# Attention and mixture of experts on one core: the causal mask moves into the row-maximum pass of the vector engine, the values' constant to the GpSimd engine

## The reference, cut to what matters

```
xa  = x @ (W_attn + lora)^T ; normalised over all tokens (batch norm), then split into q, k, v
att = softmax(causal(q k^T / sqrt(128)))
x   = LayerNorm(x + att v @ W_proj^T @ (W_proj + lora)^T)
gates = the two largest router probabilities of LayerNorm(x), made to sum to 1
x   = LayerNorm(x + sum over the two experts e of gate_e * (gelu(LN_e(x) W1_e + b1_e) W2_e + b2_e))
```

## Time and profile before

| what | value |
|---|---|
| median of 3 runs | 430.78 us (429.72 to 431.52) |
| profiled execution, its own time | 431.83 us |
| its span | 430.1 us |
| mean granted clock of PE | 0.985 |
| PE busy | 408.5 us (95%) |
| DVE busy | 282.9 us (66%) |
| ACT busy | 323.7 us (75%) |
| POOL busy | 321.0 us (75%) |

### The profile page before, as it was taken

The page is one execution under the profiler, slowest core; times in us unless marked ns, Lnnn a source line. Parts: engine busy times, 40 slices in busy tenths (PEclk is TensorE's granted clock), DMA queues, the critical chain, the costliest instruction groups (busy, mean ns, idle before and its releaser), DMA issues.

```text
span 430.1 us, 14555 instructions
## 1 busy us (share of the span) xinstructions
PE 408.5 (95%) x3490; PEld 390.8 (91%) x3490; DVE 282.9 (66%) x1612; ACT 323.7 (75%) x830; POOL 321.0 (75%) x606
## 2 busy tenths in 40 slices
PE   7998899999998999999999999999999999999980
PEld 7967787999887999999999999999999999999980
DVE  2446677899999677656555555446766666666663
ACT  1226788999988678877888888888888888888751
POOL 7000276888888888888887787748878888788885
PEclk9999999999999899999999999999999999999995
DMA  9999411111113532454543355542333333333211
GB/s 236 323 402 378 117 41 34 42 45 48 42 47 115 123 85 85 127 148 137 138 128 108 98 166 155 161 139 72 106 101 105 111 108 109 108 83 101 69 32 37
DMA packets 45490, 51.69 MB, mean 120 GB/s; under 512 B 6610, under 2 KB 37074, under 8 KB 45410
## 3 DMA queue, kind: packets, MB, share of 16 engines
q1 hardware_dynamic: 37312, 31.46, 27.0%
q0 software_dynamic: 7728, 18.51, 12.7%
q10 hardware_dynamic: 370, 0.80, 0.6%
HBM read 28.23 MB, written 21.72 MB: 116 GB/s over the span
## 4 chain that ended last, share of the span: by engine, by line
PE 65%; POOL 13%; issue 12%; DVE 5%; ACT 1%; DMA 1%; POOLq 0%; SPq 0%; DVEq 0%; ACTq 0%
PE bank L880 19%; PE bank L895 18%; POOL r_z L603 7%; POOL out L609 6%; PE bank L686 3%; PE bank L740 3%; PE bank L870 3%; PE bank L726 2%; PE bank L761 2%; PE bank L677 2%; PE bank L749 1%; PE bank L770 1%; PE bank L772 1%; PE bank L751 1%; PE bank L750 1%
## 5 line engine op out<-in xcount | busy, mean ns | idle before, releaser
L880 PE MATMUL bank<-xT 128*128 128x128 f32 x1136 | 152.1, 277 | 0.0
L895 PE MATMUL bank<-w2T,xT 128*128 x1136 | 150.2, 275 | 0.6 <-DVE yt L1476 0.6
L895 PEld LDWEIGHTS bank<-w2T,xT 128*128 128x128 f32 x1136 | 138.2, 192 | 0.8 <-issue 0.8
L880 PEld LDWEIGHTS bank<-xT 128*128 128x128 f32 x1136 | 138.7, 193 | 0.0
L932 ACT ACTIVATE xT<-w1T,zero_col 128x512 f32 x139 | 100.4, 722 | 41.2 <-issue 37.5
L1476 DVE TENSOR_TENSOR yt<-bank,b_bc 128x128 f32<-128x128 f32 x142 | 41.4, 291 | 92.7 <-PE bank L895 87.6
L609 POOL DMA_INDIRECT out<-xT,xg x71 | 75.9, 1069 | 17.1 <-issue 17.1
L596 POOL DMA_INDIRECT queue<-xT,xg x71 | 72.0, 1014 | 20.1 <-POOL idle L594 16.2
L1069 ACT ACTIVATE xT<-bank 128x512 f32<-128x512 f32 x142 | 82.0, 577 | 2.4 <-PE bank L880 2.4
L575 POOL DMA_INDIRECT queue<-x_all x64 | 62.2, 972 | 12.6 <-issue 7.9
L932 ACT ACTIVATE xT<-bank,one_col 128x128 f32<-128x128 f32 x142 | 52.1, 367 | 10.9 <-PE bank L870 4.8
(11 more groups left out here) (238 smaller groups left out, 740.1 us busy)
## 6 DMA issues: line engine op xcount, KB each, us to landing
xg<-queue SPq DMA_DIRECT2D x71, 129.5 KB, 2.2
xg<-queue SPq DMA_DIRECT2D x71, 67.5 KB, 2.0
x_all<-x SPq DMA_DIRECT2D x16, 256.0 KB, 6.1
xT<-x_t SPq DMA_DIRECT2D x8, 512.0 KB, 9.9
w1r<-w_t SPq DMA_DIRECT2D x8, 256.0 KB, 5.8
w2T<-w_t SPq DMA_DIRECT2D x8, 256.0 KB, 11.5
queue<-xT,xg POOLq DMA_INDIRECT x71
out<-xT,xg POOLq DMA_INDIRECT x71
```

Of the source, the lines that this page charges most:

```text
L880: last = mm(bank[2 + s][:, h * P:(h + 1) * P], w1c[:, (q - 1) % WR, h * P:(h + 1) * P], xgT[:, s, :], start=True, stop=True)
L895: last = mm(bank[4 + s][:, 0:P], hs[:, s, h, :], w2T[:, bass.ds(e, 1), h, :].rearrange("p a d -> p (a d)"), start=(h == 0), stop=(h == HC ...
```

## The change

Four things are changed.

1. **The mask.** PE's `start_scores` goes away. The three score products now start their own sums. `row_max` on DVE becomes two `tensor_tensor_reduce`: each adds a f32 mask tile to the scores, turns the sign, writes the result to the new SBUF tile `masked`, and takes its minimum, which is the negated row maximum. ACT's exponentials read `masked` with scale -1 and no longer PSUM. `scores(b)` waits for `row_max(b-2)`, no longer for the exponentials of b-2.
2. **The constant.** PE's `start_v` goes away. Of `cv` only the 8 router columns still go by PE: after each of the two value products a bf16 product of 8 columns with the matrix of ones. The 128 value columns are added by POOL to x's rows (`add_constant`, one `tensor_tensor` of 128 columns for each tile): for batches 0 to 17 in one go ahead of the first scatter, for batch b+18 in the scatter of batch b, one ahead of each of its two DMAs, where the memset is then 128 columns in place of 384 (batches 14 to 31 keep 384). DVE's residual waits for it (`s_xa`). The three splits of the constant are 8 columns wide and all stand ahead of `row_max(0)`.
3. **The router's logits.** Two `tensor_tensor` over both tiles become one `scalar_tensor_tensor` for each tile, both ahead of the statistics.
4. **The gate.** ACT's `gate` moves into `roots`, between the logarithms and the wait for them.

```diff
-            def start_v(b):
-                wait(pe, s_vs, b)
-                mm(bank[1][:, 0:TPB * (E + VW)], ones_b[:], cv3[:], start=True, stop=False)
-            def start_scores(b):
-                wait(pe, s_p, b - 1)
-                mm(bank[2 + b % 2][:, 0:2 * P], ident_b[:], mask_b[:], start=True, stop=False)
             def make_v(b):
+                wait(pe, s_vs, b)
                 for t in range(TPB):
-                    last = mm(bank[1][:, t * (E + VW):(t + 1) * (E + VW)], xT[:, b * T + t * P:b * T + (t + 1) * P],
-                              wvvT[:], start=False, stop=(t == TPB - 1))
+                    at = t * (E + VW)
+                    mm(bank[1][:, at:at + E + VW], xT[:, b * T + t * P:b * T + (t + 1) * P], wvvT[:], start=True,
+                       stop=False)
+                    last = mm(bank[1][:, at:at + E], ones_b[:], cv3[:], start=False, stop=True)
                 last.then_inc(s_v, 1)
             def scores(b, s):
                 pe.wait_ge(s_zs, b + 1)
+                wait(pe, s_mx, b - 1)
...
+            ADD_FIRST = 18
+            def add_constant(b, t):
+                row = x_all[:, b * TPB + t, DATA:DATA + P]
+                return pool.tensor_tensor(row, row, cv[:, E:VW], ALU.add)
...
-            def part_transfers():
+            def part_transfers(b, t):
                 pg.settle()
-                pg.did(pool.memset(idle[:, 0:3, :], 0.0))
+                later = b + ADD_FIRST
+                if later < NB:
+                    last = add_constant(later, t)
+                    if t == TPB - 1:
+                        last.then_inc(s_xa, 1)
+                    pg.did(pool.memset(idle[:, 0, :], 0.0))
+                else:
+                    pg.did(pool.memset(idle[:, 0:3, :], 0.0))
...
+            pool.wait_ge(s_cv, 1)
+            for b in range(ADD_FIRST):
+                add_to_batch(b)
...
-                v.tensor_reduce(nmax[:, s, 0:1], bank[2 + s][:, 0:P], AXX, ALU.max, negate=True)
-                v.tensor_reduce(nmax[:, s, 1:2], bank[2 + s][:, P:3 * P], AXX, ALU.max, negate=True).then_inc(s_mx, 1)
+                v.tensor_tensor_reduce(masked[:, s, 0:P], bank[2 + s][:, 0:P], mask[:, 0:P], -1.0, -MASKED, ALU.add,
+                                       ALU.min, nmax[:, s, 0:1])
+                v.tensor_tensor_reduce(masked[:, s, P:3 * P], bank[2 + s][:, P:3 * P], mask[:], -1.0, -MASKED, ALU.add,
+                                       ALU.min, nmax[:, s, 1:2]).then_inc(s_mx, 1)
...
+            def logits(b, t):
+                op(v.scalar_tensor_tensor(out=lg[:, t, :], in0=x_cols(b, t, 0, E), scalar=x_cols(b, t, ROOT, ROOT + 1),
+                                          in1=r_bias[:], op0=ALU.mult, op1=ALU.add))
```

More of the change, by code:

```diff
@@ L489, in _ @@
             pg.did(pool.memset(zero_col[:], 0.0))
-            pg.did(pool.memset(mask_b[:], 0.0))
+            pg.did(pool.memset(mask[:], 0.0))
             pg.did(pool.iota(iota_e[:], [[1, E]], base=0, channel_multiplier=0, allow_small_or_imprecise_dtypes=True))
@@ L824, in attend_step @@
                     rank(k - 4)
-                if has[-1]:
-                    start_v(ahead)
-                    start_scores(ahead)
                 if has[1]:
@@ L975, in roots @@
                                scale=1.0 + EPS_FFN).then_inc(s_ln, 1)
+                if gated is not None:
+                    gate(gated)
                 act.wait_ge(s_ln, b + 1)
@@ L1023, in attend_step @@
                 if has[2]:
-                    roots(k - 2)
-                if has[4]:
-                    gate(k - 4)
+                    roots(k - 2, k - 4 if has[4] else None)
             def gate(b):
@@ L1233, in residual @@
                 last.then_inc(s_mv6, 1)
+            def logits(b, t):
+                op(v.scalar_tensor_tensor(out=lg[:, t, :], in0=x_cols(b, t, 0, E), scalar=x_cols(b, t, ROOT, ROOT + 1),
+                                          in1=r_bias[:], op0=ALU.mult, op1=ALU.add))
             def route(b):
                 v.wait_ge(s_rr, b + 1)
-                op(v.tensor_tensor(lg[:], x_all[:, of_batch(b), 0:E],
-                                   x_all[:, of_batch(b), ROOT:ROOT + 1].to_broadcast([P, TPB, E]), ALU.mult))
-                pg.settle()
-                op(v.tensor_tensor(lg[:], lg[:], r_bias[:].unsqueeze(1).to_broadcast([P, TPB, E]), ALU.add))
+                for t in range(TPB):
+                    logits(b, t)
                 pg.settle()
@@ L1263, in first_steps @@
                 row_max(0)
-                for n in range(1, 3):
-                    split_constant(n)
-                v.sem_inc(s_cv, 1)
                 row_max(1)
@@ L1296, in attend_step @@
                     v.wait_ge(s_rr, b3 + 1)
-                    op(v.tensor_tensor(lg[:], x_all[:, of_batch(b3), 0:E],
-                                       x_all[:, of_batch(b3), ROOT:ROOT + 1].to_broadcast([P, TPB, E]), ALU.mult))
+                    for t in range(TPB):
+                        logits(b3, t)
                     made_lg = pg.n
@@ L1301, in attend_step @@
                     v.wait_ge(s_yr, b2 + 1)
-                    op(v.bn_stats(st6[:, 0, :], x_row(b2, 0)))
-                if has[3]:
-                    pg.settle(made_lg)
-                    op(v.tensor_tensor(lg[:], lg[:], r_bias[:].unsqueeze(1).to_broadcast([P, TPB, E]), ALU.add))
-                    made_lg = pg.n
-                if has[2]:
-                    op(v.bn_stats(st6[:, 1, :], x_row(b2, 1)))
+                    for t in range(TPB):
+                        op(v.bn_stats(st6[:, t, :], x_row(b2, t)))
                     made_st = pg.n
```

54 lines of the change are left out of this document (26 added, 28 removed).

## The result

The change makes the kernel slower: 439.53 us (438.65 to 440.83, 6 runs) against 431.05 (429.72 to 431.84, 6 runs), a ratio of 1.0215 [1.0197, 1.0234]. The profiled execution took 439.34 us, its span is 437.6 us, 7.5 more than before. The forecast was 431.6 with 427.5 to 434.5, so it was wrong in its size, in its sign and in its range.

A forecast was written before the change was run, and what follows sets the result against it. PE was taken to bound attention in steps 6 to 10 and 13 to 20, DVE in 21 to 27. Profiled: 431.83 + 0.9 - 0.2 + 0.15 = 432.7; median: 430.78 + 0.85 = 431.6 us, range 427.5 to 434.5.

The forecast's parts named there:

- PE's step: PE in attention: 0.23 us removed, 0.05 and 0.24 added, net +0.06 us a step, +0.9 us over about 16 steps.
- the transposes behind the ranks: PE, each step: their first weights become uncovered, priced at 0.08 us like the other two places, without a row.
- The rival of covered weights: PE pulls f32 weight loads ahead of the small products: step 2.75 us, kernel faster at 427.6 us; chance 0.24.
- DVE has 2.98 - 2.70 = 0.28 us a step to hide it: Attention steps that PE sets: DVE's added cost stays hidden behind PE, with 0.28 us a step of room.
- steps 6 to 10: Early attention steps with PE full at 4.06 us a step: counted among those PE lengthens by 0.06 us each.
- POOL's addition: One addition of 128 columns on POOL takes 0.45 us, between 0.35 and 0.63.
- DVE's own cost: DVE: fused row maximum and logits (taken as 0) net +0.02 us a step; +0.15 us over 7 DVE-set steps.
- the step that failed: POOL before the first scatter: 36 additions take 16 us (13 to 23) while it has no work; scatter late by nothing.
- The signs that I had named for being wrong: Attention trace after: PE not full in steps 13 to 20, or its step there below 2.85 us.
- Three narrow splits ahead of `row_max(0)`: Start of attention: they replace one wide split, beside PE's first scores; cost 0, between -0.3 and +0.3 us.
- The rival had the mechanism: POOL additions and DVE's two-SBUF-operand operations block each other: 434.5 us at 0.6 us a step, at most 437; chance 0.15.
- Lateness: POOL's scatters about 3 us late (at most 9), covered by 19 us: 0; rival of later experts, 5 us or more, 0.02.

The follow-up runs named there:

- tiny_last: The whole change with only 8 batches' additions first, begun behind the splits, and both 8-column products behind both value products; 443.73 us, ratio 1.003 on the second chip.
- gaps_tt: The whole change with a wait behind each of the 36 first additions and the two old logits operations; 434.15 us, ratio 1.0094 to the kernel before.
- no_first: The whole change without POOL's 36 first additions (constant left out of batches 0 to 17); 433.92 us, ratio 1.0085 to the kernel before.
- first8_tt: The whole change with old logits and only 8 batches' additions first, begun behind the splits, the others in 24 batches' scatters; 437.56 us, ratio 1.0195.
- full_again: The whole change, unaltered, run once more on the third chip; 439.75 us, ratio 1.0222 to the kernel before.
- tt_logits: The whole change with the two old tensor_tensor operations for the logits; 441.41 us, ratio 1.0266 to the kernel before.

## Why the prediction was wrong

**PE's step: the mechanism right, one term too high, and PE not alone.** Forecast 0.06 us a step more in steps 13 to 20 and a period of 2.98. Most periods there are 2.95 to 2.96 (2.92 to 2.93 before), so +0.03; three are longer (3.12, 3.01 and 3.02), and with them the piece z(14) to z(22) has grown by 0.53, 0.07 a step. That the total agrees with the forecast is in part luck. The starts in the timeline of after give the terms: the 8-column products take 0.03 each, as priced; the second value product and the first score product, each behind a small one, 0.08 more, as priced; but the transposes behind the ranks take 0.36 to the next start in place of 0.33, so 0.03 where I had put 0.08 without a row. The rival of covered weights (0.24) falls. That PE sets these steps is not shown any more: DVE has no idle time there either, and in tiny_last 0.08 a step less on PE gave 0.01. "DVE has 2.98 - 2.70 = 0.28 us a step to hide it" failed there. In steps 6 to 10 they gained 0.29 in place of losing 0.3: the fold of one expert's matrix, which nobody edited, takes 0.86 us from L697 to L698 where it took 0.94 (60.10 to 61.04, L677 to L678, before). Why is open; with the mask's part alone it is still 0.93.

**POOL's addition: right in itself.** Forecast 0.45 us (0.35 to 0.63). It is 437 ns in the mean, and in the string 0.39 (14.06 us for 36).

**DVE's own cost: the mask as forecast, the logits at the upper bound.** The fused operations cost 0.03 to 0.04 us a step (3.99 us in the seven steps of z(22) to z(29), 3.72 before) for a forecast of +0.02. The logits I took as 0 between -0.04 and +0.08. In after the pair takes 0.27 us from start to next start (115.83 to 116.10), where the two before took 0.18, 0.19 in the mean: 0.57 us in seven steps, the whole upper bound. The two make 0.8 us where the sum had 0.15. The rest of the 1.10 us by which z(22) to z(29) has grown is mostly where the cut falls: the list's long reduction, 1.12 us to the next start, lies wholly behind z(22) in after, and before only 0.67 us of it did.

```profile
102.69 1.20 DVE L1391 TENSOR_REDUCE n_h<-oh_all 128x16 f16<-128x576 f16 x1
```

```profile
110.78 1.21 DVE L1394 TENSOR_REDUCE n_h<-oh_all 128x16 f16<-128x576 f16 x1
```

The old logits, in gaps_tt, take 0.54 us less there than the new ones in after, but the piece is only 0.15 shorter: the list's casts and the statistics take more.

**The start: the step that failed.** "In the beginning 36 additions take 16 us (13 to 23) from the moment the constant is there at about 30 us, when POOL has no work". I asked only whether POOL had time for them, and who waits for POOL. I did not ask what stands beside them on DVE, although I had the mechanism as a rival and the earlier trace rows as a warning. The signs that I had named for being wrong (PE not full in steps 13 to 20, a step below 2.85 us) did not come: they looked at the wrong stage. "The start. Three narrow splits ahead of `row_max(0)` ...: 0, between -0.3 and +0.3" failed in the same place: the splits stood beside the string, so row_max(0) came 4.20 us after z(0) in place of 2.36. By no_first (2.87) 0.5 of that are the splits' new order, the other 1.3 are POOL. By the pairs of runs the string costs 5.6 us (no_first against after), of which waits between its additions save 4.4.

**The rival had the mechanism, with the wrong bound and place.** I priced blocking in steps 11 and 13 to 20, at 0.6 us a step, with "At most each addition holds DVE for its whole length". For additions one at a time that holds: first8_tt pays 0.38 us a step where DVE has no room. In steps 13 to 20 of after the additions stretch DVE too (single logits reach 465 ns, 220 in the median) and its reserve is used up (busy 23.92 of 23.92 us, 22.73 of 23.39 in the earlier trace rows), but the step grew by only 0.07, and how much of that is PE's and how much DVE's was not separated. But 36 in a row are not one addition's length: an instruction of 8 columns waited 3.96 us, some ten additions. Nothing in the trace of before showed a string, and I took a bound for one operation as a bound for any number.

The Trainium skill (SBUF — State Buffer, Who interferes with whom) says that a DVE instruction with two SBUF inputs contends with a GpSimd instruction that reads SBUF and not with one that only writes, and that one with a single SBUF input, outside the two-port modes, does not contend. The runs agree: 3964 ns beside additions, 0.36 us for the pair beside memsets, 164 ns for `ohr` with and without additions. That DVE and POOL both use `x_all` does not explain it: the one-hots and the gates' differences grew in first8_tt and do not read it. The same section says that copies and casts in their two-port mode contend with GpSimd; with memsets they took 0.30 to 0.45 us for 0.16 and 0.17.

**Lateness: covered, as said.** POOL's first scatter began at 57.5 us (50.8 before) and the 36th at 121.18 (111.5), and SP's first row loads came at 141.4, 0.5 after z(31), as they did before (132.4, 0.3 after): they followed attention and not POOL.

**The sum.** Forecast +0.85 us between medians, measured +8.5. The string is 5.6 of it. no_first's ratio leaves 0.85%, 3.7 us: 0.6 in z(0) to z(2) and 0.4 in z(4) to z(7), 0.5 and 1.0 in the long stretches, 0.2 at the end and -0.3 in steps 6 to 10 add up to 2.4 at z(31), and 0.4 is a later z(0), which differs so between executions of one kernel. The rest of about 1 us I can't place; the profiled execution of before was itself 1 us over its median, with a last piece of 14.91 us that was 13.05 to 14.34 in all the others of the first and third chips.

## What to carry to other kernels

Work that is moved to an idle engine is not free because that engine is idle: ask where both engines have their operands, what the other engine does in the same microseconds, and above all whether it comes as one unbroken string beside a critical instruction. If it must run there, put a wait between its instructions (4.4 us here for one line), or place it where the other engine has room to spare and nowhere else. And taking a small covered product from PE may uncover the weight load of the next: count the distances between starts, not the columns.

## What the runs showed of the hardware that was not expected

- A string of 36 POOL additions, issued without waits, held a DVE operation of 8 columns with both operands in SBUF for 3964 ns (2515 in full_again, 2805 in tt_logits); with a wait between the additions the longest was 465 ns. Two others with both operands in SBUF passed the same string near its beginning in 150 and 380 ns. In the same string DVE's casts and copies took 0.28 to 0.47 us, and its operations with one operand in PSUM kept their length: the two fused ones of the row maximum took 0.29 and 0.42 us at 39.54, beside the string, and 0.28 and 0.42 at 114.74, long after it.
- The stall was followed by PE's lower clock: `make_z` 1.20 us in place of 0.59 after PE had waited 3.17 us at one product. When it fell and how long it stayed low differed between two executions of the same program, which moved one piece between 13.30 and 11.95 us.
